# Rows of means and factors: written and spread from GpSimd's queue, q and k of a unit in one broadcast

## The reference

```
h = einsum('bct,bcd->bdt', x, cond_w[subject])           # a 64x64 matrix per sequence
q, k, v = h@Wq, h@Wk, h@Wv                               # 16 heads of 128
beta, gate = sigmoid(h@Wb + bb), silu(h@Wg)
q, k = silu(causal_conv4(q)), silu(causal_conv4(k))
q, k = layernorm over the 128 channels of each head, times w, plus b
S_t = (1-beta_t) S_(t-1) + beta_t v_t k_t^T ;  o_t = S_t q_t
x = x + (o*gate) @ Wo
x = x + ffn(x @ W2^T + adapter)                          # ternary weights, int8-like activations
```

## Time and profile before

| | |
|---|---|
| median of 3 runs | 2547.58 us (2545.19 to 2547.93) |
| profiled execution, its own time | 2545.06 us |
| its span, first to last instruction | 2543.3 us |
| PE busy | 2444.2 us, 96% |
| DVE / ACT / POOL busy | 1625.5 / 1073.2 / 786.1 us |
| mean granted TensorE clock | 0.984 |

### The profile page before, as it was taken

How to read it: one execution, slowest core, us unless ns; L and a number is a source line. 1 busy time by engine, 2 the same in 40 slices (tenths; PEclk the granted TensorE clock), 3 DMA queues, 4 the chain that set the end, 5 groups by cost and what they waited for, 6 DMA issues and landing times. The chain is left out here.

```text
span 2543.3 us, 38355 instructions
## 1 busy us (share of the span) xinstructions
PE 2444.2 (96%) x14263; PEld 1847.0 (73%) x14292; DVE 1625.5 (64%) x2653; ACT 1073.2 (42%) x1615; POOL 786.1 (31%) x636
## 2 busy tenths in 40 slices
PE   6889999999999999999999999999999999999996
PEld 5667777777777777777777777777777777777764
DVE  3666665676567666676556766667566676667663
ACT  4554543534444343443434434444344433444331
POOL 3465532232232222232233232232232232232241
PEclk9999999999999999999999999999999999999997
DMA  6788867576566776666676676666766577566660
GB/s 228 243 306 285 275 212 240 170 246 241 184 229 197 231 226 210 199 204 224 212 234 196 203 245 221 212 203 200 260 203 219 170 244 240 186 223 203 228 198 25
DMA packets 326962, 551.38 MB, mean 217 GB/s; under 512 B 98354, under 2 KB 122970, under 8 KB 326778
## 3 DMA queue, kind: packets, MB, share of 16 engines
q1 hardware_dynamic: 315778, 529.75, 62.6%
q10 hardware_dynamic: 11000, 19.18, 2.4%
HBM read 495.08 MB, written 53.74 MB: 216 GB/s over the span
## 5 line engine op out<-in xcount | busy, mean ns | idle before, releaser
L559 POOL TENSOR_TENSOR og_lo<-gt,og_hi 128x512 fp32r<-128x512 f32 x128 | 180.8, 1413 | 1105.2 <-ACT og_hi L1073 1105.2
L1143 PE MATMUL pj_a<-ht_hi,wg 128*128 128x512 f32 x1024 | 361.4, 414 | 16.0 <-DMA wg<-parts_g 12.7
L1143 PE MATMUL pj_a<-ht_hi,wq 128*128 128x512 f32 x1024 | 354.4, 407 | 7.2 <-issue 3.2
L837 DVE SCALAR_TENSOR_TENSOR y_q<-pj_a,conv,y_q 128x504 f32<-128x504 f32 (+2 forms) x384 | 281.1, 732 | 125.0 <-ACT y_q L1049 115.7
L1143 PE MATMUL pj_b<-ht_hi,wk 128*128 128x512 f32 x1024 | 346.3, 399 | 6.3 <-DMA wk<-parts_k 6.3
L1143 PE MATMUL ring<-wv,ht_hi 128*128 128x512 f32 x1024 | 319.8, 394 | 1.3 <-POOL wv L549 1.3
L837 DVE SCALAR_TENSOR_TENSOR y_k<-pj_b,conv,y_k 128x504 f32<-128x504 f32 (+2 forms) x384 | 281.4, 733 | 52.6 <-ACT y_k L1049 43.5
L555 POOL TENSOR_TENSOR y_k<-y_k,sq_k 128x512 f32<-128x512 f32 x128 | 171.7, 1342 | 457.8 <-DMA sq_k<-m_rows 457.2
L1143 PE MATMUL ring<-wo,og_hi 128*128 128x512 f32 x992 | 312.6, 396 | 0.0
L1143 PEld LDWEIGHTS pj_b<-ht_hi,wk 128*128 128x128 f32 x1024 | 192.1, 188 | 103.8 <-issue 49.5
L1143 PEld LDWEIGHTS pj_a<-ht_hi,wg 128*128 128x128 f32 x1024 | 198.5, 194 | 64.8 <-DMA wg<-parts_g 14.0
(11 more groups left out here) (198 smaller groups left out, 4649.5 us busy)
## 6 DMA issues: line engine op xcount, KB each, us to landing
wq<-parts_q SPq DMA_DIRECT2D x112, 512.0 KB, 4.2
wk<-parts_k SPq DMA_DIRECT2D x112, 512.0 KB, 6.3
wg<-parts_g SPq DMA_DIRECT2D x112, 512.0 KB, 6.0
wv<-parts_v SPq DMA_DIRECT2D x112, 512.0 KB, 6.5
wo<-parts_o SPq DMA_DIRECT2D x108, 512.0 KB, 6.6
sq_q<-m_rows SPq DMA_DIRECT2D x110, 256.0 KB, 3.6
sq_k<-m_rows SPq DMA_DIRECT2D x110, 256.0 KB, 4.5
sq_q<-r_rows SPq DMA_DIRECT2D x110, 256.0 KB, 3.5
```

The costliest lines, as they stand in the source:

```text
L559: G.tensor_tensor(og_lo[:, u % OG_RING, :], gt[:, u % GT_RING, :], og_hi[:, u % OG_RING, :].bitcast(F32), ALU.subtract).then_inc(S["oglo"], 1)
L837: V.scalar_tensor_tensor(out=yy[:, :, k:], in0=pp[:, :, :L - k], scalar=conv[:, i, h, 3 - k:4 - k], in1=yy[:, :, k:], op0=ALU.mult, op1=AL ...
L1143: last = T.matmul(psum, a, b, start=start and n == 0 and m == 0, stop=stop and n == len(pairs) - 1 and m == 2)
```

## The change

All issues of the rows' DMAs go to GpSimd's program, in every slot; the versions in ScalarE's and SyncE's programs and `ROWS_SP` are deleted. The tiles `sq["q"]` and `sq["k"]` become one tensor `sq_both`, in which q and k of a unit are neighbours, so that one DMA of 512 KB brings both: two broadcasts replace four. The semaphores `m_in_q0` ... `m_in_k1` become `m_in0`, `m_in1`, the same for `r_in`.

In GpSimd's even slots `send_means` comes behind the k split, `spread_means` behind the v, o and g splits, and `centre_k` behind that. In odd slots `send_rstd` and `spread_rstd` come behind all splits.

```diff
+        sq_both = sb("sq_both", [P, 2, 2, GROUP])
+        sq = {n: sq_both[:, :, i, :] for i, n in enumerate("qk")}
...
+        def pair_rows(rows, u):
+            return rows[2 * u:2 * u + 2, :].rearrange("(o x) t -> o x t", o=1).broadcast_to([P, 2, GROUP])
...
# GpSimd
+            def send_means(m):
+                pool.wait_ge(S["mean_kept"], m + 1)
+                for u in range(2 if m else 0):
+                    pool.wait_ge(S[f"m_in{u}"], 16 * m)
+                pool.dma_start(m_rows, rstd[0:P:32, :]).then_inc(S["m_out"], 16)
+            def spread_means(m):
+                pool.wait_ge(S["m_out"], 16 * (m + 1))
+                for u in range(2):
+                    for x_ in "qk" if m else "":
+                        pool.wait_ge(S[f"n_{x_}"], 2 * m - 1 + u)
+                    pool.dma_start(sq_both[:, u], pair_rows(m_rows, u)).then_inc(S[f"m_in{u}"], 16)
+            def send_rstd(m):
+                pool.wait_ge(S["rr"], m + 1)
+                for u in range(2 if m else 0):
+                    pool.wait_ge(S[f"r_in{u}"], 16 * m)
+                pool.dma_start(r_rows, rstd[0:P:32, :]).then_inc(S["r_out"], 16)
+            def spread_rstd(m):
+                pool.wait_ge(S["r_out"], 16 * (m + 1))
+                for u in range(2):
+                    pool.dma_start(sq_both[:, u], pair_rows(r_rows, u)).then_inc(S[f"r_in{u}"], 16)
...
                 if U % 2 == 0 and 2 <= U <= UNITS:
-                    centre_k(U - 2)
-                    centre_k(U - 1)
+                    send_means(U // 2 - 1)
                 for b in blocks:
                     if b[0] in "vog":
                         split_lo(b)
+                if U % 2 == 0 and 2 <= U <= UNITS:
+                    spread_means(U // 2 - 1)
+                    centre_k(U - 2)
+                    centre_k(U - 1)
+                if U % 2 and 3 <= U <= UNITS + 1:
+                    send_rstd((U - 3) // 2)
+                    spread_rstd((U - 3) // 2)
...
# SyncE's and ScalarE's loops: the calls are gone
-                if U % 2 == 0 and ROWS_SP <= U <= UNITS:
-                    send_means(U // 2 - 1)
-                if U % 2 and ROWS_SP <= U <= UNITS + 1:
-                    send_rstd((U - 3) // 2)
...
-                    if U < ROWS_SP:
-                        send_means(U // 2 - 1)
-                if U % 2 == 0 and 2 <= U < ROWS_SP:
-                    spread_means(U // 2 - 1)
-                if U % 2 and 3 <= U < ROWS_SP:
-                    send_rstd((U - 3) // 2)
-                if U % 2 and 3 <= U < ROWS_SP:
-                    spread_rstd((U - 3) // 2)
```

More of the change, by code:

```diff
@@ L121, in adaln_attn_ffn @@
     SLOTS = UNITS + 5
-    ROWS_SP = H + 4
     assert DK == P and D == 512 and NAD * RANK == P and H == 16 and L == 64 and HT == 4 and D == SET * P
@@ L153, in adaln_attn_ffn @@
         y = {n: sb(f"y_{n}", [P, Y_RING, GROUP]) for n in "qk"}
-        sq = {n: sb(f"sq_{n}", [P, 2, GROUP]) for n in "qk"}
+        sq_both = sb("sq_both", [P, 2, 2, GROUP])
+        sq = {n: sq_both[:, :, i, :] for i, n in enumerate("qk")}
         rstd = sb("rstd", [P, GROUP])
@@ L207, in adaln_attn_ffn @@
             w_hi_done w_split ring_mm0 ring_mm1 ring_mm2 ring_mm3 ring_free0 ring_free1 ring_free2 ring_free3
-            proj_q proj_k proj_g mean_made mean_kept m_out m_in_q0 m_in_k0 m_in_q1 m_in_k1
-            var scores r_out r_in_q0 r_in_k0 r_in_q1 r_in_k1 weighed
+            proj_q proj_k proj_g mean_made mean_kept m_out m_in0 m_in1
+            var scores r_out r_in0 r_in1 weighed
             tap0_q tap0_k tap_q tap_k silu_q silu_k c_q c_k gated
@@ L355, in load_keep @@
                                  rows[:, b].broadcast_to([L, HT, L])).then_inc(S[f"keep_in{u % 2}"], 16)
[L357 to L379, removed]
             def load_v(s, part):
@@ L551, in centre_k @@
             def centre_k(u):
-                pool.wait_ge(S[f"m_in_k{u % 2}"], 16 * (u // 2 + 1))
+                pool.wait_ge(S[f"m_in{u % 2}"], 16 * (u // 2 + 1))
                 c = y["k"][:, u % Y_RING, :]
@@ L840, in centre_q @@
             def centre_q(u):
-                dve.wait_ge(S[f"m_in_q{u % 2}"], 16 * (u // 2 + 1))
+                dve.wait_ge(S[f"m_in{u % 2}"], 16 * (u // 2 + 1))
                 c = y["q"][:, u % Y_RING, :]
@@ L857, in normalise @@
                 for x_ in "qk":
-                    dve.wait_ge(S[f"r_in_{x_}{u % 2}"], 16 * (u // 2 + 1))
+                    dve.wait_ge(S[f"r_in{u % 2}"], 16 * (u // 2 + 1))
                     c = y[x_][:, u % Y_RING, :]
@@ L1014, in keep_means @@
                 A.activation(rstd[:], stat[:], ACT.Identity).then_inc(S["mean_kept"], 1)
[L1016 to L1042, removed]
             def first_tap(x_, u):
```

## The result

| | before | after |
|---|---|---|
| median of the runs | 2546.39 us (2544.25 to 2547.93, 4 runs) | 2747.66 us (2743.79 to 2753.3, 4 runs) |
| ratio | | 1.079, 95% interval 1.077 to 1.081 |
| span of the profiled execution | 2543.3 us | 2745.0 us |
| mean granted clock of TensorE | 0.984 | 0.955 |

The account below looks back on a forecast made before the run. TensorE was taken as the bound, busy 2444 of 2543 us. Losses of 33, 14 and 10 less gains of 15.3 and 3 gave +39 on 2545.1, so 2584, named 2585 for the median; range 2545 to 2622.

Parts of the forecast that it names:

- The sign that the prediction itself named as wrong: Profile after: waits for the variance in the later groups would show the forecast wrong; no size given.
- The weight waits, 15.3 won: From 420 to 2440 us: TensorE's waits for wk and wg vanish, 15.3 us won, between 8 and 20.
- GpSimd's issue, 1.0 us: GpSimd's program: each DMA issue takes 1.0 us, between 0.32 and 1.3.
- The later groups, means, 0 us: Later groups: means' squares stay ready before the variance, 4 us of cover, 2 allowed; 0 us lost.
- Rival 3: Later groups: slow GpSimd trips make squares 5 us later; 1 us in each of 54 pairs, 2639 us; chance 0.12.
- The later groups, factors, 0 us: Later groups: factors reach VectorE at most 2 us later, within 3 us of cover before the scores; 0 lost.
- Group 0, the means, 33 us: Group 0: spread behind the wg split delays squares, TensorE waits before the variance; 33 us lost, between 18 and 45.
- Group 0, the factors, 14 us: Group 0, odd slots: factors' write and spread behind the splits delay the scores; 14 us lost, between 5 and 25.
- Group 0, the clock, 10 us: Group 0: matmuls run at a lower clock after nine new waits of over 2 us; 10 us lost, 0 to 20.

Follow-up runs that it names:

- e8: e1 with ScalarE issuing the merged rows in every slot and SyncE none; 2548.30 us, ratio 1.001 to the kernel before.
- e11: e1 with ScalarE issuing the means in every slot, SyncE the factors from slot 20; 2527.09 us, ratio 0.993 to the kernel before.
- e12: e6 with the write of the means moved between GpSimd's two affines; 2540.05 us, ratio 0.998 to the kernel before.
- e6: e3 with the factors given back to SyncE, so GpSimd issues only the means from slot 20; 2593.97 us, ratio 1.020 to the kernel before.
- e1: Kernel before with two merged 512 KB broadcasts instead of four of 256 KB, ScalarE and SyncE issuing as before; 2536.31 us, ratio 0.997.
- e3: Merged broadcasts, ScalarE issuing the rows up to slot 19 as before, GpSimd all rows from slot 20; 2644.77 us, ratio 1.040 to the kernel before.
- e5: e3 with the means given back to SyncE, so GpSimd issues only the factors from slot 20; 2560.07 us, ratio 1.006 to the kernel before.
- e13: e1 with GpSimd issuing the means in slots 2 to 18 at the changed kernel's places; 2598.11 us, ratio 1.020 to the kernel before.
- e14: e1 with GpSimd issuing the factors in slots 3 to 19 at the changed kernel's places; 2566.39 us, ratio 1.007 to the kernel before.
- e9: Changed kernel with e4's order and the means' write between the two affines in every slot; 2620.23 us, ratio 1.028 to the kernel before.
- e4: Changed kernel with the means' spread, centring and factors' issues ahead of the v, o and g splits; 2697.41 us, ratio 1.062 to the kernel before.
- e7: e3 with the write of the means moved between GpSimd's two affines in the later groups; 2579.50 us, ratio 1.016 to the kernel before.
- e10: e5 with the small write of the factors given back to SyncE, GpSimd still spreading them; 2548.30 us, ratio 1.001 to the kernel before.

## Why the prediction was wrong

The sign and the main mechanism of group 0 were right. The forecast was 163 us too low. Of these, 123 lie behind slot 20, where the sum had 15 us won and nothing lost and 107 were lost; 40 lie in the first 20 slots, where it had 54 us lost (33 + 14 + 10 - 3) and 94 were. The sign that the prediction itself named as wrong, waits for the variance in the later groups, came: 21 of them, 24.5 us.

**The weight waits, 15.3 won: right for the waits, not shown for the time.** None is left in the kernel after. In e8 none is left either, and nothing is gained; e11 gains 18 us.

**GpSimd's issue, 1.0 us, between 0.32 and 1.3: right, to the side of high.** The write took 0.61, the two spreads together 1.07 to 1.10.

**The later groups, means, 0 us: the step that failed.** I let GpSimd issue after the last affine, 3 us later than SyncE, and took the short end, 1.7 us plus the issue, for written to spread, "since nothing of GpSimd's own lies ahead of them". Measured, the write came 4.2 us later than before (5.0 against 0.8), and write to spread took 3.6, less than the 4.7 from SyncE. First q was 3.6 us later, where the sum allowed 2, and e12 and e6 fence the true cover: 0.6 us later than in e1 costs nothing, 2.5 us later costs 57 us. Rival 3 had late means and waits for the variance, with GpSimd's affine ahead of the write named for it, but took the lateness from a slow trip of 5.9 us; at 1 us in each of 54 pairs it gave 2639. The write's place in the program was the reason, not the transfer. What I saw and did not follow through is that the affines ahead of the write depend on the factors, so a later factor trip makes the write later again: the 30 us by which e3 exceeds e5 and e6.

**The later groups, factors, 0 us: failed by the trip of some slots, and by the cover.** "At most 2 us later" was right on average (1.3). It was read in one slot: in the kernel after, the factors are 4.3 us later in slot 3 of a group, 3.7 in slot 9 and 2.7 in slot 13. The prediction had it that rows on their own queue would not stand behind weights; e5's slot 9 shows that they do, 6.0 us for the small write with 2 MB issued ahead on SyncE's queue, 2.1 without. What was not followed through is that SyncE, held by no rows, issues these loads earlier. The cover was misread as well: the affine done at 1011.7 is that of unit U-3, that of U-4 was done at 1010.1, 3.4 us ahead of its scores. In slot 10 there is less: of e5's 4.1 us 3.0 come out as a wait, so the cover there is some 1 us, an estimate. The page of the Trainium skill that the prediction weighed (DMA: Bandwidth & Descriptors, "Latency and other measured facts") gives GpSimd's path 0.4 us more to the first byte; measured from the small write to the spread behind it, GpSimd's takes 2.1 us against SyncE's 1.7 where no large load is ahead, and 0.9 to 1.5 us more on average over all slots (2.7 to 3.3 against 1.8).

**Group 0, the means, 33 us: mechanism right, size not.** In slot 10 the spread at g + 5.3 was measured at g + 5.1, and TensorE's arrival at g + 9.4 at g + 9.6. The term that was mis-sized is spread to last square: 8.5 us taken, 10 as the end of the range, 11.8 measured to the variance (279.12 to 290.92). The first q needed 7.3 of them, where the rows from ScalarE needed 5.3. The second miss is slot 2, which I gave 0.2 us because it splits only g: TensorE waited 8.2 us there. Its write went out behind the k split at 64.65 and the spread followed at 70.75, 6.1 us for the written rows alone. The waits before the variance of the first 20 slots (slot 19's 8.5 us, which lies in the second window above, is one of them) are 64.5 us, 61.6 more than before; e13 gives 57 us for the means alone.

**Group 0, the factors, 14 us: near in the sum, partly by luck.** The waits before the scores rose by 18 us; e14 gives 25 us of time. Slot by slot the estimates were less good: slot 6 rose by 7.8 us (1.3 forecast), 8 by 3.1 (2.0), 10 by 4.4 (5.7), 12 by 5.6 (3.4), 14 by 0.3 (2.0), and slot 4 fell by 2.8.

**Group 0, the clock, 10 us: low.** 94.3 us were lost; TensorE's gaps of over 0.25 us before slot 20 add up to 126.5 us against 50.3, so some 76 are waits, and the remaining 18 are the slower matmuls behind them. Waits before the variance and the scores that are new or grew by over 2 us are 12, not nine. Behind slot 20 the same count gives 117.9 against 42.3, 76 us of waits, and 32 of slower matmuls. The clock was not in the sum there at all.

## What to carry to other kernels

When a DMA issue moves to another engine's program, write down which instructions stand ahead of it there and what they wait for, back to the source: if one of them waits for an earlier trip of the same kind, the delay feeds itself. Look at what the relieved engine issues earlier, too: here it was 2 MB of loads that came ahead of a small write. Read the trip and the cover of a wait in every kind of slot of the loop, not in one, since a mean of 1.3 us can be 4 in one slot of 16, and price a lost microsecond in each as a wait plus matmuls at the lower clock. If a change costs much, first move the call within the new program: here one line was worth 61 us, and the same gain that the change was after came from giving one of the two trips to an engine where nothing stands ahead of the write (e11).

## What the runs showed of the hardware

- A small write (four rows of 2 KB) took 1.7 us from SyncE's issue to its next one behind the wait and 2.0 to 2.2 us from GpSimd's where no large load was ahead (e1, e5). With 2 MB on SyncE's queue, their issue begun 2.3 us ahead of it, GpSimd's took 4.2 to 7.3 us: in e5 it was issued at 501.82 and its first packet moved at 505.6. The mean over all slots, 2.7 to 3.3 us, mixes the two. The 512 KB broadcasts land 5.4 to 5.8 us (median) after issue from GpSimd, 4.7 (factors, SyncE) to 4.9 (means, ScalarE) in e11.
- When one DMA brings q and k together, VectorE and GpSimd subtract at the same time: GpSimd's subtraction takes 1.75 us on average after, 1.62 in e1 and 1.70 in e11, 1.34 before. It cost e1 and e11 nothing that shows. In the slot shown above it took 1.76 us beside VectorE's 0.69 at 286.37, and a split of the same size 1.28 with VectorE idle. The Trainium skill (SBUF — State Buffer, "SBUF: two separate sides") has a VectorE instruction with two SBUF inputs and a GpSimd instruction that reads SBUF lock each other out of a shared port, the later one for the whole of the first; the trace agrees in direction, not in size, with 0.48 us added where 0.64 of VectorE's instruction were still to go.
- It goes the other way too: VectorE's scan, 0.68 us alone, took 4.33 us in e5 at 509.63 beside back-to-back subtractions and additions of GpSimd, and 4.78 and 5.84 in e9's group 0. A VectorE instruction of 2.8 us or more comes in at least six of the seven later groups of the kernel after, e3, e4, e5 and e7, and in none of the kernel before, e1, e6, e8, e10 and e12, where GpSimd does not write the factors.
- In the stretch with the lowest granted clock, 0.76 from 100 to 200 us, TensorE was busy 62 of 100 us; at 89 of 100, before, it was 0.92.
